# New order of TensorE's products, ScalarE's copies and VectorE's steps in one pass of a two-layer attention kernel

## The chip, the cores and the metric

The kernel runs on one core of a Trainium2 chip. The metric is the device time of one execution in microseconds (us), as the median of several. Lower is better.

## The reference

Two transformer blocks follow each other on x (4 sequences of 1024 tokens, 256 channels, fp32), 16 heads of 16 channels.

```python
# block 0 (shift and scale of each norm, and the gates, come from a small modulation product)
h = _ln(x) * (1 + sc_msa) + sh_msa
x = x + _self_attn(h, w_qkv, b_qkv, w_so, b_so) * g_msa        # windows of 128 tokens, rolled by 64
h = _ln(x) * (1 + sc_mca) + sh_mca
x = x + _topk_cross_attn(h, context, ...) * g_mca              # 64 keys, softmax over the 16 largest
h = _ln(x) * (1 + sc_mlp) + sh_mlp
x = x + (silu(a) * b @ w_m2 + b_m2) * g_mlp                    # a, b = halves of h @ w_m1 + b_m1, 1024 wide
# block 1
xq = _ada_ln(x, ...); xkv = _ada_ln(context, ...)
x = x + softmax(q k^T / 4) v @ Wp + bp                         # plain cross attention, 64 keys
```

## The kernel before, in words

The 4096 tokens are cut into 8 blocks of 512 (4 tiles of 128 tokens). Each block passes through four layers: 1 is self attention, 2 the cross attention with the 16 largest scores, 3 the gated linear unit, 4 the last cross attention. The program is software-pipelined over three blocks. A pass `full(a)` (a = 2 to 7) does layer 1 of block a, scores and selection of layer 2 of block c = a-1, and context values of layer 2, layer 3 and layer 4 of block b = a-2. Ahead of the six passes stand `first()` and `second()`, behind them `last()`.

All five engines run lists that are written by hand, one per engine, each in a function `full` of its own: TensorE's is made of the steps that `bank_order` lists, ScalarE copies products out of PSUM (with bias, exp, silu), VectorE does the norms' statistics, the selection, the maxima and the sums with x, GpSimd does rsqrt, adds of bias rows and softmax parts, SyncE issues all DMAs from one in-order list. PSUM's 8 banks are handed out in turn by `bank_order`: the product at place n of that list uses bank n mod 8, and `fill_wait` makes it wait until the reader of the product eight places earlier is done ("drained"). So the order decides both when an engine comes to a step and whose reader must be done before.

Names that recur:
- `("TP", b, ...)`: turned probabilities of layer 2; `("T", n, ...)`: the turn (transposition) of normalised tiles for layer n, which waits for VectorE's `normalise(n, ...)`; `("q2", ...)`, `("q3", ...)`: queries; `("S", c, ...)`: scores of layer 2, which `topk(c, t, steps)` works on; its five steps for tile t are 0 the eight largest, 1 taking these out, 2 the next eight, 3 taking these out, 4 the sum and the masking.
- `("O", 2, b)` are context values of layer 2 and `("O", 4, b)` those of layer 4, `("D", 4, b)` denominators; `("y", n, ...)` is the projection of layer n, for 512 tokens in two halves, read by VectorE's `residual(n, ...)`.
- `("A", a, w)`: self scores of window w for their maximum (`window_max`); `window(a, w)`: the maximum turned (`mT`) and scores minus maximum (`B`), whose exp ScalarE takes; `("PV", a, w)`: values of window w, divided by `window_divide`. `A3`, `mT3`, `B3` are the same for layer 4 (`last_for_max`, `last_max`, `last_scores`).
- `mlp_in(b)` makes `ua`, `ub` of layer 3. Its input is split in a rounded part `qr` and a rest `h_low`, which VectorE's `input_rest` makes of two SBUF operands; `gated_linear(b, j)` closes chunk j of 8.
- SyncE's list has, at the end of pass a, a wait until `("y", 4, b, 1)` is drained and then `store(b)` (and on odd a three loads); it then begins pass a+1 with a wait for `("y", 1, a, 1)` and `load_x(a+1)` into `xin`, which `first_moments(a+1)` waits for. This code isn't touched by the change.

## Time and profile before

| | us |
|---|---|
| median of 3 runs | 981.95 (980.56 to 983.8) |
| the profiled execution, its own time | 985.19 |
| its span (first to last instruction) | 983.3 |

The mean granted clock of TensorE is 0.974 of full speed. The page of the profile gives busy time by engine, the chain of work that ended last, and groups of instructions; a view of stretches gives the busy time of each engine in chosen stretches; the timeline lists instructions in order of time. One pass lasts 110.5 to 111.6 us.

### The profile page before, as it was taken

The numbers are of one execution on the slowest core, as the hardware profiler recorded it, in microseconds if no ns is written. First come the engines' busy times: TensorE is split into PE (matmuls) and PEld (weight loads), VectorE is DVE, ScalarE is ACT, GpSimd is POOL, SyncE is SP. The second block draws the span as 40 slices with busy tenths as digits, with TensorE's granted clock in tenths as the row PEclk, the third lists the DMA queues.
The fourth block names the chain that finished last, engine by engine and source line by source line (L and its number), as shares of the span: only waits on it lengthen the run. The fifth ranks groups of instructions, "written<-read, shape, count | busy, mean of one in ns | idle before, by whom it ended". The sixth has DMA issues, their size and how long they took to land.

```text
span 983.3 us, 22093 instructions
## 1 busy us (share of the span) xinstructions
PE 887.6 (90%) x8032; PEld 651.3 (66%) x8032; DVE 760.4 (77%) x4000; ACT 476.8 (48%) x791; POOL 303.1 (31%) x233
## 2 busy tenths in 40 slices
PE   5978878998999899998999989998999987988997
PEld 3755655685778656875778756875678754774774
DVE  3669798898689967998689877998689965996423
ACT  3356535426463557526473457526473454534414
POOL 1225534412251515222252415222152422331101
PEclk9999799999999999999999999999999999898999
DMA  8304011000100102000100102000100100000000
GB/s 314 93 23 167 2 33 51 11 2 2 60 2 1 56 24 60 12 2 3 60 1 2 55 23 62 12 1 2 55 7 1 56 18 17 1 1 1 22 1 22
DMA packets 28651, 32.81 MB, mean 33 GB/s; under 512 B 4176, under 2 KB 25600, under 8 KB 28288
## 3 DMA queue, kind: packets, MB, share of 16 engines
q1 hardware_dynamic: 28544, 31.41, 10.1%
q8 instruction: 64, 1.05, 0.4%
q14 instruction: 43, 0.35, 0.1%
HBM read 25.05 MB, written 6.36 MB: 32 GB/s over the span
## 4 chain that ended last, share of the span: by engine, by line
PE 64%; DVE 24%; ACT 8%; issue 3%; POOL 1%; DMA 1%; SPq 0%; ACTq 0%; POOLq 0%
PE bank L1593 60%; DVE left L1297 6%; DVE negm L1253 5%; DVE top L1295 4%; DVE negm L1324 2%; PE bank L1796 2%; PE bank L1611 2%; ACT hT L814 2%; ACT arena L931 1%; DVE x L1227 1%; DVE stats L1169 1%; DVE xh L1181 1%; ACT arena L888 1%; ACT rden_self L859 1%; DMA w_m<-in_w_ada 1%
## 5 line engine op out<-in xcount | busy, mean ns | idle before, releaser
L703 POOL TENSOR_TENSOR arena<-arena,topk_sum 128x1024 f32<-128x1024 f32 x32 | 61.4, 1917 | 182.8 <-DVE arena L1289 182.8
L1593 PE MATMUL bank<-w_m,arena 128*128 128x256 f32 x512 | 112.6, 381 | 2.4 <-issue 2.4
L1593 PEld LDWEIGHTS bank<-w_m,arena 128*128 128x128 f32 x512 | 96.6, 190 | 16.8 <-issue 3.2
L1297 DVE MATCH_REPLACE8 left<-top,left 128x64 f32<-128x64 f32 x512 | 99.9, 208 | 0.0
L1297 DVE MATCH_REPLACE8 left<-top,arena 128x64 f32<-128x64 f32 x512 | 99.9, 210 | 0.0
L920 ACT ACTIVATE rden<-bank,chan 128x512 f32<-128x512 f32 x64 | 44.2, 690 | 101.9 <-PE bank L1593 99.6
L868 ACT ACTIVATE arena<-bank 128x512 f32<-128x512 f32 x128 | 66.1, 602 | 48.3 <-PE bank L1593 48.3
L1253 DVE TENSOR_REDUCE negm<-bank 128x4 f32<-128x512 f32 x128 | 78.8, 682 | 13.8 <-PE bank L1593 13.2
L1295 DVE MAX8 top<-arena 128x8 f32<-128x64 f32 x512 | 67.8, 209 | 25.1 <-ACT arena L888 25.1
L692 POOL TENSOR_TENSOR exps<-arena,top 128x1024 f32<-128x1024 f32 x32 | 62.0, 1938 | 79.1 <-DVE top L1295 78.9
L881 ACT ACTIVATE exps<-exps 128x1280 f32<-128x1280 f32 x32 | 40.7, 1271 | 91.2 <-POOL exps L697 90.5
L1593 PE MATMUL bank<-qr,w_m 128*128 128x512 f32 x256 | 83.1, 405 | 0.2 <-ACT qr L824 0.2
L1593 PE MATMUL bank<-qr,m_low 128*128 128x512 f32 x256 | 81.2, 399 | 0.0
L1593 PE MATMUL bank<-h_low,w_m 128*128 128x512 f32 x256 | 70.6, 397 | 2.3 <-DVE h_low L1309 2.3
L1295 DVE MAX8 top<-left 128x8 f32<-128x64 f32 x512 | 67.8, 210 | 0.5
L1316 DVE SCALAR_TENSOR_TENSOR arena<-bank,chan,rden 128x512 f32<-128x512 f32 x64 | 47.2, 744 | 22.4 <-ACT rden L920 22.4
L1227 DVE TENSOR_TENSOR x<-bank,x 128x512 f32<-128x512 f32 x50 | 34.4, 688 | 38.2 <-PE bank L1593 38.1
L697 POOL TENSOR_TENSOR exps<-top 128x256 f32<-128x256 f32 x32 | 19.9, 621 | 135.6 <-DVE top L1295 135.6
L897 ACT ACTIVATE arena<-bank 128x512 f32<-128x512 f32 x64 | 32.4, 621 | 59.0 <-PE bank L1796 59.0
L650 POOL TENSOR_SCALAR veps<-mv 128x4 f32<-128x4 f32 (+1 forms) x32 | 7.9, 246 | 169.0 <-DVE mv L1176 162.4
L1593 PE MATMUL bank<-hT,w_qkv 128*128 128x512 f32 x128 | 58.7, 612 | 0.2 <-ACT hT L814 0.2
L1593 PEld LDWEIGHTS bank<-h_low,w_m 128*128 128x128 f32 x256 | 48.3, 189 | 14.8 <-DVE h_low L1309 3.1
(164 smaller groups left out, 1917.3 us busy)
## 6 DMA issues: line engine op xcount, KB each, us to landing
w_m<-in_w_m SPq DMA_DIRECT2D x4, 1024.0 KB, 5.8
xin<-in_x SPq DMA_DIRECT2D x4, 512.0 KB, 4.2
arena<-in_w_m SPq DMA_DIRECT2D x1, 2048.0 KB, 8.9
out<-x SPq DMA_DIRECT2D x4, 512.0 KB, 3.0
arena<-in_w_ada SPq DMA_DIRECT2D x1, 1536.0 KB, 11.3
gate<-gate_rows SPq DMA_DIRECT2D x12, 128.0 KB, 3.4
gated_bias<-gate_rows SPq DMA_DIRECT2D x12, 128.0 KB, 3.8
xin<-in_x SPq DMA_DIRECT2D x3, 384.0 KB, 3.1
```

The lines of the kernel that those rows point to most:

```text
L692: nc.gpsimd.tensor_tensor(eS, S[:, t, :].rearrange("p (h n) -> p h n", h=H), top[:, :, 0:1].to_broadcast([P, H, LC]), ALU.subtract).then_i ...
L703: nc.gpsimd.tensor_tensor(Sh, Sh, topk_sum[:].unsqueeze(2).to_broadcast([P, H, LC]), ALU.mult).then_inc(s_prob, 1)
L868: drain(nc.scalar.activation(pT_self[:, w % 2, 4 * r:4 * r + 4, :], ps(key).rearrange("p (h q) -> p h q", h=4), ACT.Exp, scale=SCORE_SCALE ...
L881: nc.scalar.activation(exps[:], exps[:], ACT.Exp, scale=SCORE_SCALE).then_inc(s_exp, 1)
L897: drain(nc.scalar.activation(pT[:, 4 * k:4 * k + 4, t * P:(t + 1) * P], ps(key).rearrange("p (h q) -> p h q", h=4), ACT.Copy), key)
L920: drain(nc.scalar.activation(sa[:, j % 2, :], ps(key), ACT.Silu, bias=chan[:, CB["m1"] + j:CB["m1"] + j + 1]), key)
L1227: drain(nc.vector.tensor_tensor(x[:, slot, tiles], ps(key).rearrange("p (t n) -> p t n", t=2), src, ALU.add), key)
L1253: drain(nc.vector.tensor_reduce(negm[:, w, r, 0:4], ps(key).rearrange("p (h n) -> p h n", h=4), AX_X, ALU.max, negate=True), key)
L1295: i = nc.vector.max(eight, scores)
L1297: i = nc.vector.match_replace(left[:, h, :], eight, scores, REPLACED)
L1316: drain(nc.vector.scalar_tensor_tensor(hid[:, j, :], ps(key), chan[:, at:at + 1], sa[:, j % 2, :], ALU.add, ALU.mult), key)
L1593: return nc.tensor.matmul(dst, lhsT, rhs, start=start, stop=stop)
```

## The change

Nothing is added or removed: the same instructions stand in another order on TensorE, ScalarE and VectorE. Core of the diff (TensorE's list repeats `bank_order`, so only one of the two is shown; the lists of a = 2 on VectorE are shortened):

```diff
 bank_order / front_and_middle(a), a > 2
         yield from probs(b)
+        yield from by_chunk("T", 2, c)
         yield from values(2, b)
-        yield from by_chunk("T", 2, c)
+        yield from by_chunk("q2", c)
         yield from project(2, b)
-        yield from by_chunk("q2", c)
 bank_order / full(a)
         yield from window(a, 0)
         yield from by_row_group("A", a, 2)
         yield from window(a, 1)
-        yield from by_row_group("A", a, 3)
         yield ("PV", a, 0)
         yield from by_chunk("T", 4, b)
+        yield from by_row_group("A", a, 3)
+        yield ("PV", a, 1)
+        yield from by_chunk("q3", b)
         yield from window(a, 2)
-        yield from by_chunk("q3", b)
-        yield ("PV", a, 1)
         yield from by_row_group("A3", b, 0)
+        yield from by_row_group("A3", b, 1)
         yield from window(a, 3)
-        yield from by_row_group("A3", b, 1)
         yield ("PV", a, 2)
         yield from by_row_group("B3", b, 0)
         yield ("mT3", b)
         yield from by_row_group("B3", b, 1)
+        yield ("PV", a, 3)
         yield from values(4, b)
-        yield ("PV", a, 3)
+        yield from project(1, a)
         yield from project(4, b)
-        yield from project(1, a)
 ScalarE
                     take_probs(b)
-                    take_cross(b)
                     act.wait_ge(s_cur_middle, 16 * (c // BLKS + 1))
                     modulated(2, c)
+                    take_cross(b)
...
                 modulated(4, b)
+                self_denominator(a, 1)
+                last_query(b)
                 window(a, 2)
-                last_query(b)
-                self_denominator(a, 1)
                 window(a, 3)
                 self_denominator(a, 2)
                 last_exps(b)
-                cross_denominator(4, b)
                 topk_exp(c, 3)
                 self_denominator(a, 3)
+                cross_denominator(4, b)
 VectorE, a > 2
                     first_moments(a)
+                    normalise(1, a, (2, c))
                     residual_moments(2, b)
-                    normalise(1, a, (2, c))
                     normalise(3, b, (1, a))
                     topk(c, 0, (0, 1, 2))
-                    take_values(a, 0)
                     input_rest(b)
-                    take_values(a, 1)
-                    topk(c, 0, (3, 4))
+                    topk(c, 0, (3,))
+                    take_values(a, 0)
+                    gated_linear(b, 0)
+                    topk(c, 0, (4,))
+                    take_values(a, 1)
+                    gated_linear(b, 1)
...
+                    gated_linear(b, 7)
+                    window_max(a, 0)
+                    topk(c, 1, (4,))
+                    topk(c, 2, (0, 1, 2,))
+                    window_max(a, 1)
+                    residual_moments(3, b, (0,))
+                    residual_moments(3, b, (1,))
+                    window_max(a, 2)
+                    normalise(4, b, (3, b))
+                    topk(c, 2, (3,))
...
+                    residual_moments(1, a, (0,))
+                    residual_moments(1, a, (1,))
+                    residual(4, b, 0)
+                    residual(4, b, 1)
+                    normalise(2, a, (4, b))
 VectorE, a == 2
-                    topk(c, 0, (0,))
                     normalise(1, a, (2, c))
-                    topk(c, 0, (1,))
+                    topk(c, 0, (0, 1,))
```

In short: the self projection goes ahead of the last one at a pass's end; the turn for layer 2 goes ahead of the context values, and its query ahead of their projection; on VectorE `residual_moments(3, ...)` comes behind one stretch of selection instead of between two, and selection steps lie elsewhere among the unit's chunks.

TensorE from the values of layer 4 at the end of a pass to the scores' query in the next, before (`vpad` and `ones_half` are a window's values, `pair_mask` and `vbd` denominators and values by head pair, `w_last,oT` the projection of layer 4, `w_so` that of layer 1, `w_co` that of layer 2, `ident,arena` the turned probabilities, `w_q` the query):

```order
L1593 MATMUL bank<-arena,pair_mask 32x512 x4
L1593 MATMUL bank<-arena,vbd 32x512 x4
L1593 MATMUL bank<-arena,vpad 32x128 x16
L1593 MATMUL bank<-arena,ones_half 32x256 x8
L1593 MATMUL bank<-w_last,oT 128x256 x8
L1593 MATMUL bank<-w_so,oT_self 128x256 x8
L1796 MATMUL bank<-ident,arena 128x128 x32
L1593 MATMUL bank<-arena,vbd 32x512 x8
L1611 MATMUL bank<-ident,xh 128x128 x8
L1593 MATMUL bank<-w_co,oT 128x256 x8
L1593 MATMUL bank<-hT,w_q 128x512 x4
```

and in the changed kernel:

```order
L1647 MATMUL bank<-arena,pair_mask 32x512 x4
L1647 MATMUL bank<-arena,vbd 32x512 x4
L1647 MATMUL bank<-w_so,oT_self 128x256 x8
L1647 MATMUL bank<-w_last,oT 128x256 x8
L1850 MATMUL bank<-ident,arena 128x128 x32
L1665 MATMUL bank<-ident,xh 128x128 x8
L1647 MATMUL bank<-arena,vbd 32x512 x8
L1647 MATMUL bank<-hT,w_q 128x512 x4
L1647 MATMUL bank<-w_co,oT 128x256 x8
```

The last window's values now stand ahead of layer 4's, the two projections and the two pairs behind the turned probabilities are swapped.

TensorE from the values of window 0 to the end of window 3, before (`qk,q_by_parity` are `A`, `ident,negm` `mT`, `q_by_parity,qk` and `mTs,head_rows` together `B`, `hT,w_last` `q3`, `kbd,qk` `A3`):

```order
L1593 MATMUL bank<-qk,q_by_parity 128x128 x16
L1593 MATMUL bank<-arena,vpad 32x128 x16
L1593 MATMUL bank<-arena,ones_half 32x256 x8
L1611 MATMUL bank<-ident,xh 128x128 x8
L1662 MATMUL bank<-ident,negm 128x128
L1593 MATMUL bank<-q_by_parity,qk 128x256 x8
L1593 MATMUL bank<-mTs,head_rows 128x128 x16
L1593 MATMUL bank<-hT,w_last 128x512 x4
L1593 MATMUL bank<-arena,vpad 32x128 x16
L1593 MATMUL bank<-arena,ones_half 32x256 x8
L1593 MATMUL bank<-kbd,qk 128x128 x16
L1662 MATMUL bank<-ident,negm 128x128
```

and in the changed kernel:

```order
L1665 MATMUL bank<-ident,xh 128x128 x8
L1647 MATMUL bank<-qk,q_by_parity 128x128 x16
L1647 MATMUL bank<-arena,vpad 32x128 x16
L1647 MATMUL bank<-arena,ones_half 32x256 x8
L1647 MATMUL bank<-hT,w_last 128x512 x4
L1716 MATMUL bank<-ident,negm 128x128
L1647 MATMUL bank<-q_by_parity,qk 128x256 x8
L1647 MATMUL bank<-mTs,head_rows 128x128 x16
L1647 MATMUL bank<-kbd,qk 128x128 x32
L1716 MATMUL bank<-ident,negm 128x128
```

`A` of window 3 moved behind the turn for layer 4, and both halves of `A3` now follow each other directly behind window 2.

VectorE at the start of a pass, before (`xin` is the loaded x, `h_low` `input_rest`, `vpad` `take_values`, `MAX` and `MATCH_REPLACE` the selection):

```order
L1169 BN_STATS stats<-xin 128x6 x4
L1176 BN_AGGR mv<-stats 128x2 x4
L1227 TENSOR_TENSOR x<-bank,x 128x512
L1169 BN_STATS stats<-x 128x6 x2
L1181 TENSOR_SCALAR xh<-xin,mv,rstd 128x256 x4
L1181 TENSOR_SCALAR xh<-x,mv,rstd 128x256 x4
L1295 MAX top<-arena 128x8 x16
L1297 MATCH_REPLACE left<-top,arena 128x64 x16
L1295 MAX top<-left 128x8 x16
L1244 TENSOR_TENSOR vpad<-bank,rows 128x8x2x16 x2
L1309 TENSOR_TENSOR h_low<-xh,qr 128x512 x2
```

and in the changed kernel:

```order
L1169 BN_STATS stats<-xin 128x6 x4
L1176 BN_AGGR mv<-stats 128x2 x4
L1181 TENSOR_SCALAR xh<-xin,mv,rstd 128x256 x4
L1227 TENSOR_TENSOR x<-bank,x 128x512
L1169 BN_STATS stats<-x 128x6 x2
L1181 TENSOR_SCALAR xh<-x,mv,rstd 128x256 x4
L1295 MAX top<-arena 128x8 x16
L1297 MATCH_REPLACE left<-top,arena 128x64 x16
L1295 MAX top<-left 128x8 x16
L1309 TENSOR_TENSOR h_low<-xh,qr 128x512 x2
```

The norm of the new block moved ahead of the two sums of layer 2, and `h_low` ahead of the values of layer 1.

## Rows read from the trace of the kernel before

**Rows 1.** The page: busy time by engine.

```profile
PE 887.6 (90%) x8032; PEld 651.3 (66%) x8032; DVE 760.4 (77%) x4000; ACT 476.8 (48%) x791; POOL 303.1 (31%) x233
```

**Rows 2.** Stretches: from:to, length, busy PE, PEld, DVE, ACT, POOL, PEclk, DMA.

```profile
434.99:477.94 42.95, 38.16 (x562) 25.98 (x561) 33.89 (x159) 23.84 (x47) 9.99 (x7) 1.00 0.04 14
477.94:545.49 67.55, 66.58 (x418) 51.22 (x416) 58.18 (x340) 34.02 (x49) 23.48 (x18) 1.00 0.05 15
545.49:589.50 44.01, 39.59 (x562) 27.51 (x561) 33.90 (x159) 23.83 (x47) 14.91 (x11) 0.96 0.14 43
```

**Rows 3.** TensorE's timeline, pass a=5: start, length, what, idle before.

```profile
482.21 1.92 PE L1593 MATMUL bank<-arena,vbd 128*32 128x512 f32 x16 [0.61 <-issue]
...
508.53 1.09 PE L1593 MATMUL bank<-h_low,w_m 128*128 128x512 f32 x4
...
531.57 14.08 PE L1593 MATMUL bank<-w_m,arena 128*128 128x256 f32 x64
```

**Rows 4.** TensorE's timeline, back stage of pass a=4.

```profile
437.61 1.17 PE L1593 MATMUL bank<-qk,q_by_parity 32*128 32x128 f32 x32 [0.88 <-DVE x L1227]
...
439.61 1.10 PE L1593 MATMUL bank<-q_by_parity,qk 32*128 32x256 f32 x13 [0.57 <-DVE negm L1253]
...
441.51 1.17 PE L1593 MATMUL bank<-qk,q_by_parity 32*128 32x128 f32 x32 [0.36 <-DVE negm L1253]
...
455.29 1.10 PE L1593 MATMUL bank<-q_by_parity,qk 32*128 32x256 f32 x13 [0.74 <-DVE negm L1324]
...
457.19 1.17 PE L1593 MATMUL bank<-kbd,qk 32*128 32x128 f32 x32 [0.36 <-DVE negm L1324]
```

**Rows 5.** ScalarE's timeline, pass a=4, the four exps of window 0.

```profile
436.75 2.07 ACT L868 ACTIVATE arena<-bank 128x512 f32<-128x512 f32 x4 [1.06 <-PE bank L1593]
```

**Rows 6.** VectorE's timeline, pass a=5.

```profile
481.50 1.38 DVE L1181 TENSOR_SCALAR xh<-x,mv,rstd 128x256 f32<-128x256 f32 x4 [1.47 <-POOL rstd L653]
...
496.13 2.13 DVE L1295 MAX8 top<-arena 128x8 f32<-128x64 f32 x16 [1.72 <-ACT arena L888]
...
501.53 2.13 DVE L1295 MAX8 top<-left 128x8 f32<-128x64 f32 x16
...
505.80 1.28 DVE L1309 TENSOR_TENSOR h_low<-xh,qr 128x512 fp32r<-128x512 f32 x2
...
527.84 1.40 DVE L1316 SCALAR_TENSOR_TENSOR arena<-bank,chan,rden 128x512 f32<-128x512 f32 x2
```

**Rows 7.** SyncE's timeline, issues of DMAs at the end of passes a=4 and a=5.

```profile
478.86 1.77 SPq L486 DMA_DIRECT2D xin<-in_x  x3
```

```profile
586.97 1.57 SPq L486 DMA_DIRECT2D out<-x  x3
...
591.46 0.43 SPq L486 DMA_DIRECT2D xin<-in_x  x1
```

**Rows 8.** VectorE's timeline, start of pass a=6.

```profile
595.94 1.41 DVE L1169 BATCH_NORM_STATS2 stats<-xin 128x6 f32<-128x256 f32 x4 [1.49 <-DMA xin<-in_x]
```

**Rows 9.** VectorE's timeline, pass a=2.

```profile
149.08 2.12 DVE L1295 MAX8 top<-arena 128x8 f32<-128x64 f32 x16 [2.08 <-ACT arena L888]
...
172.02 3.89 DVE L1309 TENSOR_TENSOR h_low<-xh,qr 128x512 fp32r<-128x512 f32 x2
```

**Rows 10.** GpSimd's and ScalarE's timelines, pass a=2.

```profile
167.99 2.37 POOL L678 TENSOR_TENSOR xin<-xin,gated_bias 128x1024 f32<-128x1024 f32 x1
170.31 3.38 POOL L678 TENSOR_TENSOR x<-x,gated_bias 128x1024 f32<-128x1024 f32 x1
```

```profile
150.82 1.17 ACT L904 ACTIVATE oT<-bank 128x512 f32<-128x512 f32 x2
```

**Rows 11.** TensorE's timeline, start of `last()`.

```profile
815.69 1.64 PE L1611 MATMUL bank<-ident,xh 128*128 128x128 f32 x8 [0.47 <-DVE xh L1181]
```

**Rows 12.** Stretches of lower granted clock (columns as in rows 2).

```profile
353.00:355.00 2.00, 2.00 (x16) 0.45 (x12) 1.63 (x17) 1.18 (x4) 0.00 (x0) 0.50 0.03 8
773.00:775.00 2.00, 2.00 (x36) 2.00 (x32) 2.00 (x6) 0.22 (x1) 0.00 (x0) 0.50 0.06 18
```

143 lines of the change are left out of this document (90 added, 53 removed).

## The prediction, made blind

> **What bounds the kernel now.** I read the page first: TensorE is busy 90% of the span, VectorE 77% [rows 1], so time can only come from TensorE's waits, and a pass has few. The view by stretches cuts one pass in two. The front stage runs from the first turned probability to the first maximum's turn (mT of window 0) and takes 67.55 us with 66.58 busy; the back stage, from there to the next pass's first turned probability, takes 42.95 with only 38.16 busy [rows 2]. So about 1 us of waits stands in front and 4.8 behind. Then I read TensorE's timeline for what it waits for, and the timelines of the engine named there. Below, "+n" is time after the first turned probability of a pass (477.94 in pass 5), and "M+n" time after its mT of window 0 (434.99 in pass 4, 545.49 in pass 5) [rows 2]. TensorE works for about 3.5 us on each of: turned probabilities, each projection of layers 1, 2, 4, each query.
>
> In pass 5 the back stage takes 44.01, at a granted clock of 0.96, against 42.95 in pass 4 [rows 2]. The 1.06 us are a stretch of some 3 us at half clock (1.2 instead of 2.4 GHz) behind the waits at M+2 to M+5; passes 3 and 7 have one too [rows 12].
>
> **The front stage, odd passes (3, 5, 7).** Now the context values wait 0.61 us for ScalarE's last copies of probabilities [rows 3]. Turning for layer 2 first fills that hole, if its norm is ready. It is: the self projection now ends 3.5 us ahead of the pass, so VectorE's sums and statistics (each half of a sum about 1.5) end at about -1.4, GpSimd's rsqrt takes 1.47 [rows 6], and the norm (1.38 [rows 6]), put behind the sums of layer 4, runs from +0.9 to +2.3; TensorE wants it at +3.5. The rest of the front follows about 0.65 earlier. Two things could take this back. First VectorE: layer 3's norm moves from ahead of the query's end to behind it, since the projection of layer 2 is now second; it ends at about +18.25. The first three selection steps take 7.5 [rows 6], so they end at +25.5 to +25.8, then `input_rest` stands first. Its copies by ScalarE are ready at +26.5. Second GpSimd: behind layer 3's norm it has two adds of a bias row (2.37), a subtraction (1.94) and the third add, 9.0 us, so from +18.35 to +27.35. Pass 2 shows what happens when `h_low` meets such an add: its two instructions take 3.89 in place of 1.28, and the add 3.38 in place of 2.37 [rows 6, 9, 10]; one engine stands still while the other runs. So I let the first half run from +27.35 to +28.0, GpSimd's 0.6 us subtraction come between, and the second half end at +29.25. TensorE wants `h_low` now at 508.53, that is +30.6 [rows 3], then at +29.9: no wait, 0.6 us to spare.
>
> The Trainium skill has this as a rule (GPSIMD Engine Reference, Key points): GpSimd shares its SBUF interfaces with VectorE and contends with VectorE instructions that have two SBUF inputs. It speaks against the new place of `input_rest`, and the 3.89 of pass 2 agrees; a sum without it would be -10.9 in place of -6.25.
>
> From `input_rest` to the end of chunk 5, VectorE works 20.8 us now (507.0 + 0.7 for values, to 528.5 [rows 6]). It loses step 4 of tile 1 (1.7) and gains the two `take_values` (1.35): 20.45. So chunk 5 ends at +49.7, ahead of TensorE's last chunk (+50.3), and the unit's projection begins 0.65 earlier than its +53.63 now (531.57 [rows 3]). **Odd front: -0.65.**
>
> **The front stage, even passes (4, 6).** Here the order on SyncE's list matters, which the diff doesn't show. The list waits for layer 4's projection, stores, and only then serves the new x. Now the last projection comes first: its sum is done at 586.97, eight transfers are issued up to 591.46, and x lands at 595.94, +6.4, which VectorE already waits 1.49 for [rows 7, 8]. Swapped, layer 4's sum is done at +0.9 instead of -2.5, so the same list starts 3.4 later and x lands at +9.9. Ahead of odd passes only one store is in front, and x is issued at 478.86, +0.9, in 1.77 [rows 7]; there it lands at about +6, and its norm is done at +10.6, not wanted before +13.3.
>
> In even passes: statistics 1.8, rsqrt 1.5, norm 1.4, so the norm ends at +14.5 and the turn at +15.05 in place of +14.25. VectorE is held in front of layer 2's sums by this norm: sums 3.4, rsqrt 1.5, norm 1.4, ends +20.8; three selection steps to +28.3; GpSimd's adds to +29.8; `h_low` 29.85 to 30.5, then 31.1 to 31.75, where TensorE wants it near +31, a wait of 0.7 to 1.1. With 20.45 chunk 5 ends at +52.2, the last silu and chunk take 1.7, window 1's scores for the maximum need that bank and take 1.2: the projection begins at +55.2 against +53.63. **Even front: +1.55.** Were the two engines not to hold each other up, `h_low` would end at +29.6, chunk 5 at +50.05, and the projection would begin at +53.8: 1.4 less in each.
>
> **The back stage.** Term by term, in pass 4's times.
> - A of window 2 waits 0.88 for the sum of layer 3 [rows 4], which VectorE reaches late, behind two selection steps. Now all of that selection stands ahead, the sum follows the product at once (M+0.9): gone. But B of window 1, at 439.61 = M+4.62 now, then waits for ScalarE's exps of window 0, which end at 438.82 = M+3.83 [rows 4, 5]; with 0.14 it starts at M+3.97. **-0.65.**
> - A of window 3 waits 0.36 [rows 4] for banks of window 2's maximum; with values and a turn ahead of it, not any more. **-0.36.**
> - Both halves of A3 now stand behind window 2, and the second uses the four banks of window 2's B. B fills at M+16.8, ScalarE's four exps take 2.07 [rows 5], to M+19.0, while the second half could start at M+17.9. A wait of 1.1 instead of 0.36 [rows 4]. **+0.75.**
> - B of window 3 waits 0.74 for `last_max` now [rows 4], and about 0.7 then. **0.**
> - Window 3's values ahead of layer 4's denominators cover the last 0.3 of ScalarE's exps. **-0.3.** The projection of layer 1 has its last division at M+34.2 and starts at M+35, and the divisions of layer 4 end at M+37.4, before their projection at M+38.5: no wait.
>
> Sum: **-0.6** per pass.
>
> **Passes 2 and `last()`.** In pass 2 VectorE idles 2.08 before its first step of 2.12, and layer 1's norm stands behind it [rows 9]; now the norm goes into the idle time and its turn ends near 151.2, not 155.1. Of these 3.9 us not all arrives. ScalarE's copies end at 152.0 [rows 10], so the projection of layer 2 ends at 155.6, the self inputs at 162.6; layer 3's norm ends there too. Then GpSimd's three adds and the gate weights (to 172.6) meet the masking and `input_rest`, which ends at 173.2 instead of 175.9 [rows 9]. **-2.7**, bounds 0 and -4.6 (no meeting, 1.9 more). Its back stage gives -0.6. `last()` starts like a pass: its turn starts at 815.69 and lasts 1.64 because the norm is late [rows 11]; now it can start 1.1 earlier and a chain through scores and selection follows. **-1.1**, bounds 0 and -1.3.
>
> **Sum.** Three odd passes (-0.65 - 0.6) = -3.75; two even ones (+1.55 - 0.6) = +1.9; pass 2 -3.3; `last()` -1.1: -6.25. Half-clock stretches: three of the five passes 3 to 7 have one now; the waits in a pass fall only from 4.8 to about 4.2, and the new ones at M+18 to M+21 (1.1 and 0.7) are as dense as those at M+2 to M+5 (0.88 and 0.57). I take three again, term 0, bounds -3.2 (none) and +3.2 (all six). The profiled execution's 985.19 (span 983.3 and 1.9 around it) becomes 978.9; against the median 981.95, which lies 3.2 below it, **975.7**.
>
> **Rivals.**
> - *The two engines don't hold each other up, or half-clock stretches go.* 4.7 (2 x 1.4 + 1.9) or 3.2 less, or a part of both: 968 to 972.5. For: pass 4 has no stretch with the same waits. Against: the 3.89 of pass 2.
> - *The clock falls in every pass.* Behind the waits at M+18 to M+21 and the pair at M+26 to M+28: +3.2, 979.0. For: pass 3 fell at M+28 already [rows 12]. The Trainium skill (TensorE: Matmul & The Clock Gate, on psum-queue depth-cycling) says that frequent short idles between groups of products can make the clock oscillate; the trace shows it in three passes of five.
> - *The waits only change places.* Each cover I count on (T2 in the hole, values ahead of A) gives way to a bank or copy I didn't see: 980 to 984.
> - *Slower: x comes later still.* In even passes each us that x is late is a us of TensorE, since the norm blocks VectorE ahead of layer 2's sums. All terms but the even fronts give -9.35, so these must cost 6.1 each for +2.9 in all: x must land 4.6 us later than my +9.9 in both, or odd passes, with 2.7 us of room (+10.6 against +13.3), must lose too. The transfers behind x then contend, or the store holds the queue. At +16 the fronts cost 7.65 each: 988. Against: the queue's order and amounts are those of now, only shifted, and now they land 9.0 us after the sum.
>
> **Chances.** Forecast (972.5 to 978.9) 0.46; better (968 to 972.5) 0.22; clock falls everywhere 0.11; change of places 0.11; slower 0.10. 0.3% (2.9 us, about what a measurement can tell) puts the borders at 979.0 and 984.9. Faster: 0.46 + 0.22, and 0.02 of the clock's case, which lies on the border; slower 0.10 and 0.01 of the change of places; same 0.19. The range 968 to 983.5 leaves out the slower case and a little at the low end.
>
> **What would show it.** Right: no idle ahead of the context values, and none by VectorE's sum ahead of A of window 2; B of window 1 at M+4.0; a wait of about 1.1 at A3's second half; x's landing and `first_moments` at about +10 in passes 4 and 6, with front stages near 69.1 there and 66.9 in odd passes; back stages near 42.3 where the clock holds; `h_low` above 0.68 us an instruction in most passes. Wrong: front stages equal in odd and even passes, back stages at or above 42.95 at full clock, or more than three half-clock stretches.

## The result and the profile after

The changed kernel takes 972.58 us (median of 5 runs, 967.75 to 973.56) against 981.95 for the kernel before (5 runs beside it, 979.77 to 986.33): the ratio is 0.9891, 95% interval 0.987 to 0.9913. Run again later, beside 11 runs of the kernel before (median 982.64), it gave a ratio of 0.9864 (0.9826 to 0.9903): one of these six executions, 981.57 us, was a slow one of the kind that all ratios here leave out, the median of the other five is 968.82, and the medians below are taken the same way. So the medians differ by 9.4 and by 13.8 us, and the two intervals overlap between 9.5 and 12.8. The prediction said 975.7, within 968.0 to 983.5, and faster with a chance of 0.70: the sign was right, the gain 3.1 us too small by the first timing and 7.6 by the second.

The profiled execution of the kernel after is the fastest of the first five, 967.75 us with a span of 965.9. The page's line of busy time, to be held against [rows 1]:

```profile
span 965.9 us, 22093 instructions
PE 875.2 (91%) x8032; PEld 645.4 (67%) x8032; DVE 763.0 (79%) x4000; ACT 473.5 (49%) x791; POOL 306.8 (32%) x233
```

The instructions are the same in number. TensorE is busy 12.4 us less; a part of its "busy" time before was thus waiting that the records count to a product, or time at half clock. And 2.7 us of the difference between the two profiles lie where nothing was changed. From the first maximum's turn of `second()` to pass 2 the profile of before takes 45.95 us at a mean granted clock of 0.86. The other profiles take 43.3 there (44.5 in experiment 5; that of experiment 10, doubled as a whole, isn't counted), and experiment 6 has the same code up to this point. First before, then experiment 6:

```profile
97.50:143.45 45.95, 37.31 (x476) 27.84 (x477) 39.48 (x230) 20.66 (x40) 22.46 (x16) 0.86 0.03 8
```

```profile
98.13:141.40 43.27, 34.20 (x476) 25.73 (x476) 39.38 (x230) 20.55 (x40) 22.48 (x16) 0.93 0.03 8
```

The view by stretches, cut as in [rows 2] at the first turned probability and at the maximum's turn of window 0, for passes 4, 5 and the front of 6:

```profile
359.76:427.74 67.98, 67.38 (x418) 51.13 (x416) 56.91 (x318) 34.53 (x49) 23.11 (x17) 1.00 0.12 34
427.74:469.36 41.62, 37.17 (x562) 25.80 (x561) 36.37 (x179) 22.84 (x46) 11.18 (x9) 1.00 0.01 2
469.36:536.18 66.82, 66.52 (x417) 51.18 (x416) 56.27 (x318) 34.56 (x49) 23.09 (x17) 1.00 0.08 23
536.18:577.80 41.62, 37.18 (x561) 25.80 (x560) 36.47 (x179) 22.85 (x46) 16.08 (x13) 1.00 0.10 33
577.80:646.65 68.85, 67.40 (x417) 51.14 (x416) 56.91 (x318) 34.53 (x49) 23.09 (x17) 1.00 0.13 34
```

Odd front stages take 66.8 us, even ones 68 to 69, the back stage 41.62 at full clock in place of 42.95. The wait of 0.61 ahead of the context values [rows 3] is gone. TensorE's timeline in the back stage of pass 4 (M is 427.74 here), to be held against [rows 4]:

```profile
429.30 1.12 PE L1647 MATMUL bank<-qk,q_by_parity 32*128 32x128 f32 x32
...
431.81 1.10 PE L1647 MATMUL bank<-q_by_parity,qk 32*128 32x256 f32 x13 [1.14 <-ACT arena L868]
...
436.19 1.17 PE L1647 MATMUL bank<-qk,q_by_parity 32*128 32x128 f32 x32
...
442.70 0.27 PE L1716 MATMUL bank<-ident,negm 128*128 128x128 f32 x1
...
443.81 0.67 PE L1647 MATMUL bank<-mTs,head_rows 32*128 32x128 f32 x16
...
446.71 1.17 PE L1647 MATMUL bank<-kbd,qk 32*128 32x128 f32 x32 [1.29 <-ACT arena L868]
...
448.71 1.10 PE L1647 MATMUL bank<-q_by_parity,qk 32*128 32x256 f32 x13 [0.57 <-DVE negm L1324]
```

A of window 2 (429.30) and A of window 3 (436.19) wait for nothing. B of window 1 starts at M+4.07 behind ScalarE's exps; the second half of A3 waits 1.29 at M+18.97. VectorE's first moments in passes 4, 5 and 6 show when x lands, to be held against [rows 8]:

```profile
369.37 1.41 DVE L1169 BATCH_NORM_STATS2 stats<-xin 128x6 f32<-128x256 f32 x4 [7.42 <-DMA xin<-in_x]
475.97 1.41 DVE L1169 BATCH_NORM_STATS2 stats<-xin 128x6 f32<-128x256 f32 x4 [4.43 <-DMA xin<-in_x]
588.29 1.40 DVE L1169 BATCH_NORM_STATS2 stats<-xin 128x6 f32<-128x256 f32 x4 [8.30 <-DMA xin<-in_x]
```

That is +9.6 and +10.5 in the even passes, and +6.6 in the odd one.

### The profile page after: what moved, and what is told of

It is laid out like the page before. It is cut to its first block, busy times and chain, and to the rows that moved or that the text cites. A ratio compares the mean times of both kernels' runs of the same rounds, so it can differ in the third digit from the quotient of the medians.

```text
span 965.9 us, 22093 instructions
## 1 busy us (share of the span) xinstructions
PE 875.2 (91%) x8032; PEld 645.4 (67%) x8032; DVE 763.0 (79%) x4000; ACT 473.5 (49%) x791; POOL 306.8 (32%) x233
## 3 DMA queue, kind: packets, MB, share of 16 engines
q1 hardware_dynamic: 28544, 31.41, 10.2%
## 4 chain that ended last, share of the span: by engine, by line
PE 66%; DVE 22%; ACT 5%; issue 3%; DMA 2%; SPq 1%; POOL 1%; ACTq 0%; POOLq 0%
PE bank L1647 62%; DVE left L1297 6%; DVE top L1295 3%; DVE negm L1324 3%; PE bank L1665 2%; DVE negm L1253 2%; PE bank L1850 2%; ACT arena L868 2%; DVE arena L1316 1%; DVE stats L1169 1%; DVE h_low L1309 1%; SPq L486 1%; DVE x L1227 1%; DVE xh L1181 1%; DMA xin<-in_x 1%
## 5 line engine op out<-in xcount | busy, mean ns | idle before, releaser
L1253 DVE TENSOR_REDUCE negm<-bank 128x4 f32<-128x512 f32 x128 | 79.4, 692 | 12.8 <-PE bank L1647 12.7
L1647 PEld LDWEIGHTS bank<-qr,w_m 128*128 128x128 f32 x256 | 48.9, 191 | 12.5 <-issue 0.5
```

The lines of the kernel that those rows point to most:

```text
L1253: drain(nc.vector.tensor_reduce(negm[:, w, r, 0:4], ps(key).rearrange("p (h n) -> p h n", h=4), AX_X, ALU.max, negate=True), key)
L1647: return nc.tensor.matmul(dst, lhsT, rhs, start=start, stop=stop)
```

## Experiments

Each was timed beside 9 to 11 runs of the kernel before (medians 982.3 to 983.5), and each ratio is to that kernel. Experiments 1 to 4 ran on one chip, 5 to 8 on a second, 9 to 11 on a third, 12 on a fourth; the kernel after was timed again only in experiment 8. "Back stage" without more is its length at full clock in passes 3 to 7.

**1. Only the turn** (`e1_turn_only`). The kernel before with this on TensorE, and ScalarE's and VectorE's lists to match (not shown):

```diff
         yield from probs(b)
+        yield from by_chunk("T", 2, c)
         yield from values(2, b)
-        yield from by_chunk("T", 2, c)
+        yield from by_chunk("q2", c)
         yield from project(2, b)
-        yield from by_chunk("q2", c)
...
-        yield from project(4, b)
         yield from project(1, a)
+        yield from project(4, b)
```

> The kernel before with only the edits at the turn of a pass: the self projection ahead of layer 4's, the turn of layer 2 ahead of the context values, the next tile's query ahead of layer 2's projection, ScalarE's and VectorE's orders to match. The back stage stays as before. Theory (the turn and the back stage add up, the gain is the back stage's): odd front stages -0.65 us each, even ones +0.4 to +1.3 since x lands at about +10 instead of +6.4, last() -1 to -2.5; the back stage waits as before (A of window 2 about 0.9 us, B of window 1 about 0.6, A of window 3 about 0.35) and takes 42.95 us, about 44 where the clock falls to half. Together -0.5 to -3 us: about 979 to 981.5. Rival (the turn is the change's gain, because layer 1's norm comes earlier and takes the half-clock stretches with it): -6 us or more, about 974 to 976, and no half-clock stretch in the back stages of passes 3 to 7.

Measured: 999.62 us, ratio 1.017 (1.0142 to 1.0198). Neither: 17 us slower than before. The odd front stages are as the theory had them (67.01), the even ones (69.9) 1 us above its range, with x at +10.5. The back stages take 45.1, and 46.8 in passes 4 and 6. TensorE's row at the end of pass 4, and VectorE's four rows ahead of it:

```profile
470.48 0.69 DVE L1268 TENSOR_TENSOR oT<-bank,rden 128x512 f32<-128x512 f32 x1 [2.24 <-ACT rden L913]
471.77 0.69 DVE L1268 TENSOR_TENSOR oT<-bank,rden 128x512 f32<-128x512 f32 x1 [0.60 <-ACT rden L913]
...
473.55 1.16 DVE L1289 SCALAR_TENSOR_TENSOR arena<-left,exps 128x1024 f32<-128x1024 f32 x1
474.63 0.41 DVE L1259 TENSOR_TENSOR oT_self<-bank,rden_self 128x256 f32<-128x256 f32 x1
...
475.14 5.38 PE L1593 MATMUL bank<-w_so,oT_self 128*128 128x256 f32 x16 [2.20 <-issue]
```

The self projection (475.14) needs window 3's division (`oT_self`, 474.63), and VectorE still made it last, behind layer 4's two divisions (`oT`) and a step of selection. TensorE stood 2.20 us in every one of these passes, and in passes 4 and 6 the projection then ran at half clock for 3.4 us (5.38 for 16 products, where layer 4's 16 take 3.72 in the next experiment). I had left the order of the divisions with the other half.

**2. Only the back stage** (`e2_back_only`). The kernel before with the reordered back stage, the order of the divisions included (shortened):

```diff
         yield from by_row_group("A", a, 2)
         yield from window(a, 1)
-        yield from by_row_group("A", a, 3)
         yield ("PV", a, 0)
         yield from by_chunk("T", 4, b)
+        yield from by_row_group("A", a, 3)
...
-        yield from values(4, b)
         yield ("PV", a, 3)
+        yield from values(4, b)
...
-                cross_divide(4, b)
-                topk(c, 3, (4,))
                 window_divide(a, 3)
+                topk(c, 3, (4,))
+                cross_divide(4, b)
```

> The kernel before with only the edits of the back stage: layer 3's sums right behind the first steps of selection, values of windows 0 and 1 and layer 4's turn ahead of the scores of window 3, both halves of A3 ahead of window 3, values of window 3 ahead of layer 4's. The turn stays as before. Theory: each of six back stages is 1.33 us shorter at full clock (41.6 instead of 42.95), so -8 us, front stages at 67.55 as before; with the three half-clock stretches left 974, without them (if the waits at M+2 to M+5 bring them) 971. Rival (the back stage's 1.33 came from the turn, because layer 1's projection ahead of layer 4's covers the divisions): -0.6 a pass, 978.

Measured: 999.59 us, ratio 1.0172 (1.0144 to 1.0199): the mirror image. Front stages 67.55 as before; now layer 4's projection is first and its divisions are last:

```profile
468.67 1.28 DVE L1268 TENSOR_TENSOR oT<-bank,rden 128x512 f32<-128x512 f32 x2
...
470.00 3.72 PE L1594 MATMUL bank<-w_last,oT 128*128 128x256 f32 x16 [2.02 <-DVE oT L1268]
```

The granted clock fell more often as well: at M+21 in passes 4 to 7, and in passes 5, 6 and 7 also behind the new wait. These three have back stages of 48.5, where pass 3, at full clock, has 43.7. This stretch is in pass 5, from the wait of 0.57 for the banks of window 3 on:

```profile
565.00:572.00 7.00, 6.47 (x84) 4.79 (x84) 5.29 (x36) 2.34 (x5) 3.05 (x3) 0.52 0.01 2
```

**3. x first** (`e3_load_first`). The kernel after, SyncE's list only:

```diff
+                if a > 2:
+                    drained_wait(sp, ("y", 1, a - 1, 1))
+                    load_x(a, xin[:])
                 if a % BLKS == 0 and a > 2:
...
                     load(w_so[:], wv("w_so"), s_w[0])
                     load_modulations(cur_front, s_cur_front, batch)
+                if a > 2:
+                    drained_wait(sp, ("y", 4, a - 3, 1))
+                    store(a - 3)
```

> The kernel after with one list changed, SyncE's: the new x is loaded as soon as layer 1's sum has left its buffer, and the wait for layer 4's projection, the store and the constants of layers 1 and 2 come behind it. Theory (x late behind the list is what even front stages lose): x lands at about +6 or earlier in every pass, the 7.4 and 8.3 us idle of VectorE's first moments fall below 5, the front stages of passes 4 and 6 come down from 67.98 and 68.85 to 66.84 as in the odd ones: -3.1 us, 969.5. Rival (another thing holds even fronts, the constants of the batch or VectorE's order): x is early and the even fronts stay above 67.9, 972.5. Second rival (x meets other transfers or the store comes late enough that something waits for it): not faster than the kernel after, 972.5 to 975.

Measured: 971.44 us, ratio 0.9875 (0.985 to 0.99). In the trace the theory holds to the digit: all five front stages take 66.84 or 66.85, and x is there when VectorE comes:

```profile
363.04 1.41 DVE L1174 BATCH_NORM_STATS2 stats<-xin 128x6 f32<-128x256 f32 x4 [0.50 <-DMA xin<-in_x]
```

The median does not show the 3 us: in passes 3 to 7 this profiled execution had three half-clock stretches in its back stages (44.76, 43.24, 43.22 in passes 4, 5, 6 in place of 41.63), the first one of the kernel after none. Against that kernel's medians, 972.58 and 968.82 on other chips, no gain is settled. What is shown is what holds the even fronts.

**4. The third bias add early** (`e4_bias_early`). The kernel after, GpSimd's list only:

```diff
                 if a > 2:
+                    add_bias(2, c)
                     layer_rstd(1, a)
...
                 if a > 2:
                     subtract_max(c, 0)
-                add_bias(2, c)
+                else:
+                    add_bias(2, c)
```

> The kernel after with GpSimd's third add of a bias row ahead of layer 1's rstd from pass 3 on, so that GpSimd has ended or is at another place when VectorE forms h_low. Theory of the prediction (VectorE and GpSimd hold each other up at h_low, 1.4 us a pass arrive at the projection): h_low back near 1.28 us from 2.2 to 3.2, front stages 1 us or more shorter, 967. Rival (h_low is held up but TensorE has room there; the hold-up costs nothing): h_low short again and the time within 1 us of 972.6. Second rival (the add, moved ahead, holds layer 1's norm up by 2.4 us): front stages longer, 974 to 977.

Measured: 969.56 us, ratio 0.9863 (0.9836 to 0.989). `h_low` of pass 4 on VectorE, first in the kernel after, then here:

```profile
387.40 3.20 DVE L1309 TENSOR_TENSOR h_low<-xh,qr 128x512 fp32r<-128x512 f32 x2
```

```profile
390.05 1.27 DVE L1311 TENSOR_TENSOR h_low<-xh,qr 128x512 fp32r<-128x512 f32 x2
```

With the add gone from beside it, `h_low` is 1.9 us shorter. The front stages are hardly: 66.84 in odd passes as after, 68.92 and 68.24 in even ones, where x lands at +10.8 and +10.1. The kernel after's two profiles have 67.98 to 69.73 with x at +9.6 to +11.4, 0.99 us of front for each us of landing; at these landings that line gives 69.2 and 68.5. So the early add is worth 0.2 to 0.3 us in an even pass, about the wait of 0.34 us by the last chunks (at +52.9 and +53.8), which went. By the traces the first rival is nearest: the hold-up is real and TensorE had room for most of it. The time alone, 3.0 below the 972.58 that the rival named and 0.7 above the kernel after's second median, doesn't decide.

**5. The turn with its divisions** (`e6_turn_with_divisions`). Experiment 1 and also

```diff
-        yield from values(4, b)
         yield ("PV", a, 3)
+        yield from values(4, b)
...
-                cross_denominator(4, b)
                 topk_exp(c, 3)
                 self_denominator(a, 3)
+                cross_denominator(4, b)
...
-                cross_divide(4, b)
+                window_divide(a, 3)
                 topk(c, 3, (4,))
-                window_divide(a, 3)
+                cross_divide(4, b)
```

> The kernel before with the turn of the pass as in the turn-only run, and with what that run had left out: ScalarE's denominators and VectorE's divisions of window 3 ahead of those of layer 4, and TensorE's values of window 3 ahead of layer 4's. Theory (the two projections and the two divisions must stand in one order; the 2.20 us wait ahead of the self projection and the half clock behind it were made by the cut, not by the turn): the wait is gone, back stages 42.6 to 42.95 us at full clock instead of 45.1 to 46.8, front stages about 67.0 (odd) and 68 to 69.9 (even); -1 to -2 us against the kernel before, 980 to 982. Rival (the turn is bad whatever the divisions do, by x late and VectorE's older order of the front): 988 or more. Second rival (the turn alone brings most of the change's -10): 974 or less.

Measured: 978.24 us, ratio 0.9949 (0.993 to 0.9969), 21 us less than experiment 1 and a little below the 980 to 982 expected. The 2.20 us are gone; pass 5:

```profile
544.46:586.85 42.39, 37.88 (x561) 26.00 (x560) 34.77 (x163) 23.51 (x47) 16.11 (x13) 1.00 0.10 33
```

**6. The back stage without them** (`e7_back_without_divisions`). Experiment 2 with the three places of experiment 5 as before the change.

> The kernel before with the back stage reordered as in the back-only run, but with the divisions, the denominators and the values of window 3 and of layer 4 in the order of before. Theory: the 2.02 us wait ahead of layer 4's projection is gone; back stages 41.6 to 41.9 us at full clock instead of 42.95, front stages 67.55 as before; -7 to -8 us against the kernel before plus 0 to 3 from half-clock stretches: 974 to 978. Rival (the waits of 1.29 and 0.57 us at M+19 to M+21 bring the half clock in every pass, as they did in four of five in the back-only run): stretches of 3 to 7 us there, back stages 43.2 to 45, 980 or more. If e6 and e7 add up to the whole change: their differences to the kernel before sum to about -10 us.

Measured: 975.24 us, ratio 0.9919 (0.9902 to 0.9936). Front 67.55, back 42.09, for pass 4:

```profile
362.17:429.72 67.55, 66.58 (x417) 51.22 (x416) 56.42 (x325) 34.55 (x49) 23.51 (x18) 1.00 0.09 27
429.72:471.81 42.09, 37.46 (x562) 25.78 (x561) 35.50 (x173) 23.09 (x46) 10.00 (x7) 1.00 0.04 14
```

-4.4 (experiment 5) and -7.4 us (this one) make -11.8; the whole change measured -9.4 and, on the chip of these two, -13.8. Cut in the right place, the two halves add up within what the timings can tell, and better in the profiles. The turn takes 0.56 off each back stage, the rest 0.86, together 1.42 against 1.33.

**7. x first and the add early** (`e5_both`).

> The kernel after with both SyncE's list changed (x ahead of the store) and GpSimd's third add of a bias row ahead of layer 1's rstd. Theory (even fronts 66.85 from the early x, and no wait at chunk ends): all front stages 66.85, 968 to 969.5 as far as half-clock stretches allow. Rival (the add holds up layer 1's norm, since x is early and nothing covers it): front stages at or above 67.5, 972 or more.

Measured: 967.68 us, ratio 0.9851 (0.9825 to 0.9877). In passes 3 to 7 all front stages take 66.83 to 66.85, and two back stages have a stretch of half clock. The time is 0.3 below the expected range. The kernel after, timed beside it on the same chip, has a median of 968.82, only 1.1 more, and the executions overlap (965.6 to 972.84 here, 964.95 to 976.87 there). So the gain of the two edits is shown in the front stages and not in the time.

**8. The kernel after again** (`after_again`), unchanged.

> The kernel after, unchanged, run beside the others on the same chip, to see which of its differences to them lie in half-clock stretches. Theory: same front stages (66.84 odd, 68.0 to 68.9 even) and back stages (41.62 at full clock) to 0.1 us; what differs is how many back stages of passes 3 to 7 have a stretch of 1.6 or 3.1 us at half clock behind the waits at M+19 to M+21: 1 to 3 here, none in the first profile; 970 to 974. Rival (the stretches belong to the order of the other kernels and after has none): none again, and a span of 966.

Measured: 968.82 us, with executions from 964.95 to 976.87, where the eleven of the kernel before lie between 980.66 and 986.4. The profiled one took 975.0. Its odd fronts are 66.85, its back stages of passes 3 to 7 41.63, 43.24, 43.22, 44.70, 43.23: four of five have a stretch, more than the one to three expected. Here is the one of pass 6, which begins 1.9 us behind the end of A3's wait of 1.29, at the end of the next one of 0.56:

```profile
670.00:676.00 6.00, 5.92 (x80) 4.68 (x80) 4.83 (x35) 2.06 (x4) 0.00 (x0) 0.50 0.01 3
```

Its even fronts are 69.01 and 69.73, since x came at +10.6 and +11.4. In pass 6 one issue ahead of it took 1.49 us where it took 0.58 in the first profile; in pass 4 x was issued only 0.35 later than there and landed 1.0 later. The rival (no stretches in this kernel) falls.

**9. A3's second half behind window 3 again** (`e8_a3_split`). The kernel after with

```diff
         yield from by_row_group("A3", b, 0)
-        yield from by_row_group("A3", b, 1)
         yield from window(a, 3)
+        yield from by_row_group("A3", b, 1)
```

> The kernel after with one edit of its back stage undone: the second half of A3 stands behind window 3 again, as before the change. Theory of the prediction's term (+0.75 us a pass for the two halves together: a wait of 1.29 at the second half against 0.36 and a little of the next one): the 1.29 is gone, 0.7 us less at full clock in a back stage (40.9 in place of 41.62), six times, so about -4 us against the kernel after. Theory of the clock (the stretches of 1.6 or 3.1 us at half clock begin at that wait): they become rarer or shorter too, and the runs lie closer together than the 965 to 982 of the kernel after; together 964 to 968. Rival (the waits only change places: window 3's banks and last_max come as late as before): back stages of 41.6 to 42, the time within 1 us of the kernel after, about 972.

Measured: 973.36 us, ratio 0.9895 (0.9868 to 0.9921); back stage 41.40, only 0.2 less. The rival holds: the waits change places. TensorE's rows with a wait, from M+19 on, pass 4:

```profile
444.11 1.10 PE L1647 MATMUL bank<-q_by_parity,qk 32*128 32x256 f32 x13 [1.15 <-ACT arena L868]
...
450.87 0.50 PE L1647 MATMUL bank<-mTs,head_rows 32*128 32x512 f32 x4 [0.69 <-ACT mTs L926]
...
452.81 1.09 PE L1647 MATMUL bank<-qk,kbd 32*128 32x512 f32 x5 [1.45 <-DVE oT_self L1259]
```

Window 3's B now waits for the same exps, and the last one, 0.76 in the kernel after, is 1.45 and put down to window 2's division. Half-clock stretches came in three of five passes all the same.

**10. Both of 7 and 9** (`e10_both_a3_split`).

> The kernel after with the early x, the early bias add and the second half of A3 behind window 3. Theory (the three add up): all front stages 66.85 and back stages 0.7 us shorter than 41.63 at full clock, so about 4 us below the 967.68 of the first two: 963 to 965. Rival (the waits only change places in the back stage): 967 to 968.

Measured: 970.14 us, ratio 0.9866 (0.9838 to 0.9894), not faster than experiment 7 (on another chip), and 2 us above even the rival's time. Its only profile is of an execution that took more than twice as long (last section), so no stage can be read. The theory falls; the rival is nearest, not shown.

**11. Window 1's values as cover** (`e9_values1_as_cover`). Experiment 7 with

```diff
-        yield ("PV", a, 1)
         yield from by_chunk("q3", b)
         yield from window(a, 2)
         yield from by_row_group("A3", b, 0)
+        yield ("PV", a, 1)
...
-                self_denominator(a, 1)
                 last_query(b)
                 window(a, 2)
+                self_denominator(a, 1)
```

> The kernel after with the early x and the early bias add of the run before (967.68), and the values of window 1 moved from ahead of the query of layer 4 to between the two halves of A3, so that 1.9 us of products cover the 1.29 us wait for ScalarE's exps of window 2. Theory: that wait is gone, but the query starts 1.9 us earlier and may wait for ScalarE's turned norm; the net is between -1.3 and +0.5 us a back stage, 41.63 to 40.9 likeliest; 963 to 967. Rival (the query waits as long as is won): back stage 41.6 and 968. Theory of the clock: with a hole fewer at M+19 there are fewer half-clock stretches there.

Measured: 1007.08 us, ratio 1.0248 (1.0228 to 1.0269). None of the theories. VectorE's division of window 1 stood where it had been, ahead of two steps of selection and `last_max`, and its denominators now come late. VectorE's row and TensorE's wait for `last_max` in pass 4, then 10 us at half clock behind the beginning of such a wait, which every pass from 3 to 7 has (back stages of 49.0 to 49.3):

```profile
457.49 0.42 DVE L1266 TENSOR_TENSOR oT_self<-bank,rden_self 128x256 f32<-128x256 f32 x1 [6.30 <-ACT rden_self L866]
...
462.38 2.09 PE L1654 MATMUL bank<-kbd,qk 32*128 32x128 f32 x32 [5.82 <-DVE negm L1331]
```

```profile
459.50:469.50 10.00, 6.70 (x93) 5.84 (x97) 9.57 (x53) 1.67 (x4) 3.83 (x2) 0.50 0.01 2
```

**12. The same with the division moved** (`e11_values1_with_division`).

```diff
                     window_max(a, 3)
-                    window_divide(a, 1)
                     topk(c, 2, (4,))
                     topk(c, 3, (0,))
                     last_max(b, (0,))
+                    window_divide(a, 1)
                     last_max(b, (1,))
```

> The run with the values of window 1 as cover (1007), with VectorE's division of window 1 moved as well: from ahead of two steps of selection and last_max to between the two halves of last_max. Theory (the 5.82 us were VectorE standing in front of that division, whose denominators ScalarE now forms only behind its exps of window 2, with last_max queued behind): the 5.82 is gone, the 1.29 too since 1.9 us of products cover it, back stages 40.3 to 41.0 us at full clock in place of 41.63, front stages 66.85; against the 967.7 of the early x with the early bias add, -4 to -7: 961 to 965. Rival (the waits only change places, as with the second half of A3 behind window 3): another wait of 1 us or more between M+19 and M+29, back stages 41.4 to 42, 967 to 970.

Measured: 966.35 us (965.97 to 968.92), ratio 0.9836 (0.9808 to 0.9863), the lowest median here, though above the 961 to 965 expected, and its interval overlaps that of experiment 7. In passes 3 to 7 the 5.82 and the 1.29 are both gone, a wait of 0.74 is left at M+19.8, and the back stage takes

```profile
540.18:580.63 40.45, 37.12 (x561) 25.77 (x560) 36.33 (x179) 22.85 (x46) 16.10 (x13) 1.00 0.14 43
```

Of the 7 us that six such stages should give against experiment 7, the median shows 1.3. The profile says where they went: the six back stages together take 253.8 us, those of experiment 7 252.9. Two have a stretch of half clock (42.05, 42.04), and that of pass 2 takes 48.36 in place of 41.70. Pass 2 has a list of its own on VectorE, and in it the division of window 1 was not moved; TensorE waits for `last_max` there as in experiment 11:

```profile
230.17 2.09 PE L1654 MATMUL bank<-kbd,qk 32*128 32x128 f32 x32 [4.12 <-DVE negm L1331]
```

## Why the prediction was near, and where it was off

**The odd front (-0.65): right.** The three measure 66.84, 66.82 and 66.85, that is -0.7. The layer-3 unit's projection starts at +52.9 where +52.98 was worked out. Both profiles of the kernel after agree.

**The even front (+1.55): the step is right, its size moves.** It says that SyncE's list serves x later because layer 4's sum is now the last thing ahead of the store. Landing was put at +9.9; it was +9.6, +10.5, +10.6 and +11.4 in the two profiles, and the fronts +0.43, +1.30, +1.46 and +2.18, in the order of the landings. Experiment 3 turned the list round and these fronts came down to 66.85. So the cause is shown. The size was put too high for another reason: by the line through the four landings (experiment 4) a landing at +9.9 costs +0.7, not +1.55, and the difference is the price of the contention at `h_low`, below. The slower rival (x at 4.6 us later than +9.9) had the right mechanism and never the amount.

**Contention at `h_low`: right that it happens, priced too high.** `h_low` takes 3.20 in passes 4 and 6, where it took 1.28 as in pass 5 [rows 6], and experiment 4 brings 1.27 back by moving GpSimd's add. The Trainium skill's rule (GPSIMD Engine Reference, Key points), that GpSimd shares its SBUF interfaces with VectorE, agrees with this. In odd passes `h_low` takes 2.18, and 2.15 with the add moved, because another of GpSimd's instructions took its place: in pass 5 of the kernel after the first half of `h_low` ends at +27.75, 0.54 behind the end of the add, and in experiment 4 at +28.14, 0.54 behind the end of the multiply of the gates. The prediction let 1.4 us of an even pass hang on this; 0.2 to 0.3 did. In pass 2 `h_low` takes 4.54 and the add beside it 3.38, where before it was 3.89 and 3.38 [rows 9, 10].

**The back stage (-0.6): the step that failed, in size.** At full clock it is -1.33 in every pass from 3 on. Term by term, from start to start in the rows of pass 4:
- B of window 1 at M+3.97: M+4.07. -0.55 in place of -0.65.
- A of window 3, -0.36: -0.42, and +0.10 at the turn ahead of it.
- A3's two halves, +0.75 (with 0 for window 3's B): +1.29 for the wait, less 0.59 in window 3, which is +0.70.
- Window 3's values ahead of layer 4's denominators, -0.3: -0.46, from the gap in the middle of layer 4's products (466.14 to 467.34 in the rows below, where the step is 0.86 now) and its neighbour.
- What I had not seen: **window 2's turned maximum, -0.59.** I had put nothing there. The rows of the kernel before, ScalarE's and TensorE's:

```profile
445.37 1.43 ACT L814 ACTIVATE hT<-bank,cur_back 128x512 f32<-128x512 f32 x2
446.69 0.27 ACT L864 ACTIVATE mTs<-bank 128x128 fp32r<-128x128 f32 x1
```

```profile
445.42 0.27 PE L1662 MATMUL bank<-ident,negm 128*128 128x128 f32 x1
...
447.02 0.67 PE L1593 MATMUL bank<-mTs,head_rows 32*128 32x128 f32 x16 [0.25 <-ACT mTs L864]
447.62 3.70 PE L1593 MATMUL bank<-hT,w_last 128*128 128x512 f32 x8
...
466.14 1.07 PE L1593 MATMUL bank<-arena,vbd 128*32 128x512 f32 x8
467.34 1.07 PE L1593 MATMUL bank<-arena,pair_mask 128*32 128x512 f32 x8
```

ScalarE copied layer 4's turned norm (1.43) ahead of the 0.27 copy that window 2 needs. With the query of layer 4 between them, those copies are done long before. From the turn (mT) to the product behind the unit it was 2.20 us, now 1.61 (442.70 to 444.31). Its row shows 0.25 of idle only; the rest is hidden in the product before, which is recorded as busy. These terms make -1.22 of the -1.33, and the query of layer 4 itself, 3.54 from its start to the next product's in place of 3.63, another -0.09. No experiment took one of them alone, but the two halves of the change divide them: without window 3's values they are -0.85, and experiment 6 has -0.86; window 3's values are -0.46 of the -0.56 of experiment 5. Six stages at 0.73 more than forecast are 4.4 us.

**Pass 2 (-3.3): right in its step, too small at full clock.** From its first turned probability to the first `h_low` product it takes 27.13 us in place of 30.84. To the maximum's turn of window 0 it takes 67.2, with a half-clock stretch at +30, and 65.6 in the two profiles, against 69.35, so -2.2 and -3.7 where -2.7 was forecast. The 69.35 moves too: the profiles of experiments 1, 2, 5 and 6, whose pass 2 begins in before's order, have 68.21 to 69.05; against the mean of these five, 68.6, it is -3.0. Its back stage takes 43.23, with a half-clock stretch, and 41.69, against 42.96.

**`last()` (-1.1): too small, beyond its bound of -1.3.** It takes 169.0 to 169.2 us in all five profiles that have the new turn and were looked at for it (the kernel after twice, experiments 4, 5 and 7), against 171.7, and 171.5 in experiment 6, which has the old turn: -2.5. The term that I worked out is there: the turn of layer 2 is through at +4.46 in place of +5.70 (-1.24), and the chain through scores and selection carries that on. The other half is clock. Less work falls into the half-clock stretch behind the wait for that chain, some 0.7. The last 0.6 lie at the second such stretch, behind a wait of 2.86 for layer 4's norm: from this norm's turn to the scores for layer 4's maximum it is 8.92 us before (885.23 to 894.15) and 8.30 after (868.42 to 876.72), and the stretch there is recorded as 6.8 us long before and in experiment 6, and as 3.4 in the five with the new turn.

**The clock (0, bounds -3.2 to +3.2): the number of stretches moves from execution to execution, and each costs more than was put.** Over the five profiles of kernels with the back stage of after (the two of the kernel itself, experiments 3, 4 and 7), 0, 4, 3, 1 and 2 of the five back stages of passes 3 to 7 had a stretch, each costing 1.5 to 3.1 us where 1.06 was read from pass 5 of before: 0 to 7.9 us an execution, 3.8 on average. In pass 2, front and back, they cost another 0 to 4.7, 2.1 on average. The profile of before had three of 1.1 us, 3.3 in all. So the term is -3.3 to +4.6 for passes 3 to 7 alone, +0.5 on average, and +2.6 with pass 2; and one of its signs of being wrong, more than three stretches, showed in the second profile. The first two profiles differ by 17.4 us, where the medians differ by 9.4 and 13.8.

**The sum, with what was measured:** odd fronts -2.1, even fronts +2.7 (the mean of two profiles), six back stages -7.9, the front of pass 2 -3.0, `last()` -2.5, together -12.8 with passes 2 to 7 of the new order at full clock. The stretches bring +2.6: -10.2, against -9.4 and -13.8 measured. This takes it that the usual execution of before has its three stretches. It was profiled once, but the numbers speak for it: the profiled execution lay 3.2 above the median, 2.7 of that are the unchanged stretch of `second()`, and its mean granted clock, 0.974, becomes 0.977 when the 6.8 us of half clock which it has more there are taken off. The median of the mean clocks of the 42 executions of before beside the experiments is 0.977. This last step is worked out and not seen.

So the prediction's -6.25 was near in part by luck. At full clock it lacked some 6.5 us, most of them the back stage's size (4.4 at six stages), and the clock, for which it had 0, gave 2.6 of them back. The first median, 972.58, lies at the lower edge of its forecast (972.5 to 978.9), the second, 968.82, in the range of the rival "the two engines don't hold each other up, or half-clock stretches go", and neither of that rival's reasons is what happened. Of "the clock falls in every pass" the mechanism was seen, though not in every pass.

## What to carry to other kernels

Where two products change places on the bottleneck engine, the work that each waits for must change places with them on every other engine: each half of this change was worth +17 us alone when the projections and the divisions of window 3 and layer 4 stood in different orders, and -4 and -7 when they went together. Experiment 11 is the same mistake with window 1's division, and pass 2 of experiment 12 once more. A reordering is read unit by unit, from one product's start to the next one's, before and after; the idle time in brackets leaves out waits that the records book as a longer product. And where the clock falls in some executions and not in others, one profile is no comparison: count the stretches first, then compare stages at full clock.

## What the runs showed of the hardware

- The stretches at half clock begin behind the same few waits, yet not in every pass. In passes 3 to 7 of the five profiles with the back stage of after, TensorE waits equally in all 25 passes; in six the clock fell at M+21, behind waits of 1.29 and 0.57 us, in four at M+28.6, behind waits of 0.69 and 0.77. In experiment 2, with the same waits and a further one of 2.02 us 16 us later, it fell at M+21 in four passes of five and behind the further one in three of these, which cost 4.8 us each (48.5 against 43.7). What decides in a single pass these runs don't show.
- VectorE and GpSimd hold each other up in both directions. In the kernel after `h_low` takes 3.20 and the add beside it its usual 2.36; with the add moved, `h_low` takes 1.27 and GpSimd's small subtraction takes the loss (0.61 to 1.58):

```profile
390.21 1.58 POOL L697 TENSOR_TENSOR exps<-top 128x256 f32<-128x256 f32 x1 [0.85 <-DVE top L1297]
```

- One of the six executions of experiment 10, the profiled one, took 2237.91 us, the other five 965.31 to 974.12. In it TensorE's products took twice their time and more (835 ns for a mean of 399 in the kernel before), while VectorE's instructions did not (209 for 208). This trace holds no record of the granted clock at all, and the 1.00 that is printed for it stands for that lack; whether the clock was low stays open, and so does the cause. Two rows of its groups:

```profile
L1654 PE MATMUL bank<-qr,m_low 128*128 128x512 f32 x256 | 183.1, 835 | 0.0
L1304 DVE MATCH_REPLACE8 left<-top,left 128x64 f32<-128x64 f32 x512 | 99.8, 209 | 0.0
```
